# Depthwise convolution of both images on TensorE, by band matrices over image rows, before the first attention

## The chip, the cores and the metric

The kernel runs on one core of a Trainium2 chip. The metric is the device time in microseconds (us) from start to end of one launch: the median of 3 runs. Five engines work side by side, each on its own stream of instructions: TensorE (PE: matrix products, with its weight loads shown apart as PEld), VectorE (DVE), ScalarE (ACT), GpSimd (POOL) and SyncE (SP), which here issues all DMA transfers. They meet through semaphores.

## The reference

The input is two images `x` of 64 channels by 96 x 96 pixels in float32. Each is normalized over all its values, convolved channel by channel with the sum of a 3x3, a 5x5 and a 7x7 kernel, gated, projected, added to itself, normalized again, and passed through a full softmax attention over its 9216 pixels.

```
h = group_norm1(x, n1_g, n1_b)
f = dwconv(h, w3, b3) + dwconv(h, w5, b5) + dwconv(h, w7, b7)
g = sigmoid(conv1x1(f, gate_w, gate_b))
x = x + conv1x1(f * g, proj_w, proj_b)
h = group_norm1(x, n2_g, n2_b)
q, k, v = conv1x1(h, q_w, q_b), conv1x1(h, k_w, k_b), conv1x1(h, v_w, v_b)
attn = softmax(einsum("bnc,bcm->bnm", q, k) * C ** -0.5)
return x + einsum("bnm,bmc->bnc", attn, v)
```

## The kernel before, in words

Partition 64 h + c holds channel c of the upper (h = 0) or lower (h = 1) half of an image, 4608 pixels. There is no scheduler: every engine's program is written out by hand, engine by engine, and the order of the code is the order on the engine. SP's queue too is in written order, and a wait in it holds back all transfers behind it.

The program has these stages:

- **Prologue.** SP loads image 0, the parameters (`prm`) and the weight matrices. DVE takes the statistics (`x_stats`, L816) and computes the scale and shift (`norm`, L691 to L707); ACT (`pad_half`, L569) and DVE (L823) write the normalized image with a border of zeros into `hp`.
- **Convolution of image 0.** The three kernels are one 7x7 kernel of 49 taps. DVE adds up 17 taps (L844, L846). PE does 32 (`tap_sums`, L1045): diagonal 32x32 matrices `diag`, one for each tap and each group of 32 partitions, 16 of them side by side in the array (4 row groups x 4 column groups), over 10 chunks of 480 or 384 pixels. ACT moves each chunk's four partial sums out (L589), `fold_sums` (L1056) adds them up on PE, ACT takes the result out (L580), DVE adds it to its own (L832).
- **Gate to attention.** Nine chunks of 512 pixels go through gate (L1075), sigmoid (ACT L604), product (POOL L461), projection (L1092) and sum (DVE L862); then come the second statistics, h (ACT L608, DVE L877), the matrices Q, K and V (L1125, L1119), and 36 looks for the row maxima of the first query block (PE L956, DVE L714). The first of these looks waits for `QM`, a transfer on SP's queue. In the same stretch image 1 is loaded, its statistics are taken on DVE and it is normalized into `hp` (L569); ACT ends the stretch with the first tap of image 1 (L639).
- **Attention.** There are 18 query blocks of 512 queries in an image, and 36 key pairs (`p`) in a block. For a pair PE makes 1024 scores per partition in two PSUM banks (`scores`, L940): six matmuls of fp16 keys on queries (high by high, low by high, high by low), and two of `one16` on the third query row that subtract the row's maximum. ACT takes the exponential (L490). PE weighs V with it (L949), POOL and DVE add up E's two halves (L413, L730), and PE and DVE look ahead for the next block's maxima (L956, L714). At the end of a block DVE moves its sum out (`sums_out`, L737), once per block. In the image named in `SEEDED` (image 1), ACT writes the maxima into the odd pair's score banks beforehand (`seed`, L528, for 17 of the 36 pairs), and PE then leaves out the two `one16` matmuls of that pair.
- **Convolution of image 1, during the attention of image 0.** ACT multiplies a strip of `hp` by a tap (`make_tap`, L536), POOL adds it to `f` (`add_tap`, L427), about 20 such units in a block. In the last block DVE does 28 units by itself (`late_tap`, L774). The gate of image 1 waits for the last of them.

```
            def is_seeded(b, p):

                return b in SEEDED and p % 2 == 1 and p >= 3
```

## Time and profile before

| | before |
|---|---|
| median of 3 runs | 3034.27 us (3029.96 to 3035.54) |
| the profiled execution: its time, its span | 3029.67 us, 3027.9 us |
| granted TensorE clock, mean | 0.986 |
| busy in the span: PE, DVE, ACT, POOL | 2883.5, 2666.0, 2179.2, 2237.5 us |
| first gate matmul of image 0 | 158.29 us after the start |
| first scores of image 0, of image 1 | 251.09, 1717.06 us |

The span is the time from the first to the last instruction of the profiled execution. The stages are best told apart by instructions that occur once in each of them: the first gate matmul, the first scores, the copy that ends a block.

### The profile page before, as it was taken

What the parts mean: (1) busy time and instruction counts of PE and PEld (TensorE: products, weight loads), DVE (VectorE), ACT (ScalarE), POOL (GpSimd) and SP (SyncE); (2) the same over time, 40 slices, a digit from 0 to 9 for tenths busy, and PEclk for the clock granted to TensorE, in tenths of its full rate; (3) what the DMA queues carried; (4) which work ended last, traced back from release to release, by engine and by line L of the source; (5) the groups of instructions that cost most, each with busy time, mean ns of one, the idle gap of its engine ahead of it and who ended that gap; (6) DMA issues with size and microseconds to landing.
All of it is one profiled execution on the core that took longest, in us unless ns stands there. A gap on an engine that the chain in (4) does not pass through costs nothing.

```text
span 3027.9 us, 56969 instructions
## 1 busy us (share of the span) xinstructions
PE 2883.5 (95%) x20913; PEld 984.0 (32%) x20913; DVE 2666.0 (88%) x3096; ACT 2179.2 (72%) x2442; POOL 2237.5 (74%) x1754
## 2 busy tenths in 40 slices
PE   5878999999999999999997899999999999999998
PEld 2323333333333333333332333333333333333332
DVE  8577899999999999999987899999999999999994
ACT  1156677777777777777764678888888888888887
POOL 1045999999999999999996466666666666666666
PEclk9889999999999999999998999999999999999999
DMA  1020000000000000000001100000000000000000
GB/s 38 3 72 8 8 10 10 10 10 10 10 10 10 10 10 10 10 10 10 8 5 26 24 8 10 10 10 10 10 10 10 10 10 10 10 10 10 10 12 4
DMA packets 30978, 37.16 MB, mean 12 GB/s; under 512 B 6896, under 2 KB 29936, under 8 KB 30064
## 3 DMA queue, kind: packets, MB, share of 16 engines
q1 hardware_dynamic: 30704, 33.56, 4.6%
q8 instruction: 165, 2.70, 0.4%
q14 instruction: 109, 0.89, 0.1%
HBM read 9.94 MB, written 9.44 MB: 6 GB/s over the span
## 4 chain that ended last, share of the span: by engine, by line
PE 75%; DVE 7%; issue 7%; POOL 5%; ACT 4%; DMA 1%; SPq 0%; POOLq 0%; ACTq 0%; DVEq 0%
PE ps L949 32%; PE ps L940 29%; PE ps L956 10%; POOL accA L413 5%; DVE mxp L714 4%; PE ps L1045 3%; DVE ps L730 1%; ACT E L490 1%; ACT tapped L536 1%; PE ps L972 0%; ACT QQ L589 0%; DVE accB L737 0%; PE ps L1125 0%; ACT QS L520 0%; DVE ps L727 0%
## 5 line engine op out<-in xcount | busy, mean ns | idle before, releaser
L413 POOL TENSOR_TENSOR accA<-accA,E 128x512 f32<-128x512 f32 x1224 | 1574.5, 1286 | 458.9 <-ACT E L490 384.3
L490 ACT ACTIVATE E<-ps,bnd 128x1024 f32<-128x1024 f32 x1296 | 1391.0, 1110 | 566.4 <-PE ps L940 469.8
L714 DVE TENSOR_REDUCE mxp<-ps 128x1 f32<-128x1024 f32 x1296 | 1573.8, 1218 | 215.8 <-PE ps L956 191.8
L949 PE MATMUL ps<-E,x 128*64 128x512 f32 x5184 | 1268.2, 605 | 0.5 <-ACT pvb L500 0.5
L940 PE MATMUL ps<-QS,KK 64*128 64x512 f16 x7776 | 1056.4, 377 | 14.0 <-ACT mseed L521 10.1
L730 DVE TENSOR_TENSOR ps<-ps,E 128x512 f32<-128x512 f32 x1260 | 869.0, 690 | 46.6 <-ACT E L490 46.3
L956 PE MATMUL ps<-KK,QM 64*128 64x512 f16 x2592 | 500.8, 383 | 20.7 <-DVE mxp L714 17.6
L940 PEld LDWEIGHTS ps<-QS,KK 64*128 64x128 f16 x7776 | 374.0, 94 | 437.2 <-ACT E L490 24.8
L427 POOL TENSOR_TENSOR f<-f,tapped 128x576 f32<-128x576 f32 x356 | 505.3, 1420 | 0.0
L949 PEld LDWEIGHTS ps<-E,x 128*64 128x64 f32 x5184 | 310.8, 136 | 550.5 <-issue 394.9
L940 PE MATMUL ps<-QS,one 64*128 64x512 f16 x1980 | 377.4, 377 | 0.0
L956 PEld LDWEIGHTS ps<-KK,QM 64*128 64x128 f16 x2592 | 125.4, 93 | 693.4 <-DVE mxp L714 564.9
L528 ACT ACTIVATE ps<-mseed 128x1024 f32<-128x1024 f32 x306 | 314.6, 1028 | 28.9 <-ACT E L490 1.1
L536 ACT ACTIVATE tapped<-hp,prm 128x576 f32<-128x576 f32 x356 | 274.9, 772 | 0.0
L940 PEld LDWEIGHTS ps<-QS,one 64*128 64x128 f16 x1980 | 97.3, 94 | 117.5 <-issue 1.3
L461 POOL TENSOR_TENSOR f<-f,E 128x512 f32<-128x512 f32 x18 | 23.0, 1289 | 149.3 <-ACT E L604 149.3
L1045 PE MATMUL ps<-hp,KK 32*32 32x480 f32 (+1 forms) x2560 | 94.7, 637 | 27.6 <-ACT x L580 19.8
L418 POOL TENSOR_TENSOR accA<-E 128x512 f32<-128x512 f32 x36 | 46.8, 1300 | 97.7 <-ACT E L490 97.7
L589 ACT ACTIVATE QQ<-ps 128x480 f32<-128x480 f32 (+1 forms) x40 | 18.9, 559 | 102.2 <-PE ps L1045 102.2
L746 DVE RECIPROCAL rec<-rsum 128x64 f32<-128x64 f32 x144 | 77.3, 541 | 11.4 <-issue 8.5
L846 DVE SCALAR_TENSOR_TENSOR f<-hp,prm,f 128x4608 f32<-128x4608 f32 x16 | 80.3, 5019 | 0.6
L1045 PEld LDWEIGHTS ps<-hp,KK 32*32 32x32 f32 x2560 | 49.9, 109 | 70.8 <-issue 33.0
(105 smaller groups left out, 855.6 us busy)
## 6 DMA issues: line engine op xcount, KB each, us to landing
QS<-QQ SPq DMA_DIRECT2D x144, 64.0 KB, 2.0
x_scratch<-x SPq DMA_DIRECT2D x4, 1152.0 KB, 13.2
QM<-QQ SPq DMA_DIRECT2D x72, 64.0 KB, 2.0
xst<-x_scratch SPq DMA_DIRECT2D x72, 64.0 KB, 2.2
out<-ot SPq DMA_DIRECT2D x72, 64.0 KB, 2.0
xs<-in_x SPq DMA_DIRECT2D x2, 720.0 KB, 8.8
xs<-in_x SPq DMA_DIRECT2D x2, 648.0 KB, 5.9
xs<-in_x SPq DMA_DIRECT2D x2, 576.0 KB, 10.8
```

The lines of the kernel that those rows point to most:

```text
L413: nc.gpsimd.tensor_tensor(accA[:, n % 2, :], accA[:, n % 2, :], e, ALU.add).then_inc(adda_free, 1)
L427: nc.gpsimd.tensor_tensor(to, to, tapped[:, u % NTAPPED, :], ALU.add).then_inc(tap_added, 1)
L490: nc.scalar.activation(flat(E[:, slot_of(n % 2, p), :, :]), flat(ps[:, S_BANK + 2 * buf:S_BANK + 2 * buf + 2, :]), ACT.Exp, scale=bnd[:, 6 ...
L528: nc.scalar.activation(ps[:, S_BANK + 2:S_BANK + 4, :], mseed[:].unsqueeze(1).to_broadcast([P, 2, CH]), ACT.Copy).then_inc(seeded, 1)
L536: nc.scalar.activation(tapped[:, u % NTAPPED, :].rearrange("p (y x) -> p y x", x=W), window(t, s * SROWS, SROWS), ACT.Copy, scale=wc[:, t: ...
L714: nc.vector.reduce_max(flat(mxp[:])[:, v:v + 1], flat(ps[:, bank:bank + 2, :]), AX.X).then_inc(mx_free, 1)
L730: nc.vector.tensor_tensor(ps[:, SUM_BANK, :], ps[:, SUM_BANK, :], e, ALU.add).then_inc(addb_free, 1)
L846: chain(nc.vector.scalar_tensor_tensor(out=f3, in0=window(t, 0, HR), scalar=wc[:, t:t + 1], in1=f3, op0=ALU.mult, op1=ALU.add))
L940: a = nc.tensor.matmul(ps[:, S_BANK + 2 * (p % 2) + t, :], of[rows], QS[rows, par, part, :], start=(k == 0 and seeds is None), stop=(k == ...
L949: a = nc.tensor.matmul(ps[C * t:C * t + C, ACC_BANK, :], V[:, t, p, :], E[:, slot_of(par, p), t, :], start=(p == 0), stop=(p == NPAIR - 1) ...
L956: a = nc.tensor.matmul(ps[:, bank + t, :], QM[rows, half, qt * P:(qt + 1) * P], KH[rows, kc * CH:(kc + 1) * CH], start=True, stop=True)
L1045: a = nc.tensor.matmul(ps[GRP * g:GRP * g + GRP, NGRP * (c % 2) + r, 0:CROWS[c] * W].rearrange("p (y x) -> p y x", x=W), diag[rows, t, :], ...
```

## The change

The convolution of both images is moved ahead of everything else and is done on PE alone.

- The image comes in a second layout, made by the host (`x_rows`): image rows on partitions, in four windows of 24 rows with 3 rows more on each side, a window in each group of 32 partitions; channels and columns lie along the free axis (`xr`, 64 x 102 values per image and partition).
- For each channel and each of the 7 tap columns PE builds a band matrix of 32 x 24 (`bands`): 26 matmuls of 448 columns, moved out by ACT in 8 steps (`take_bands`). The bias and the effect of the border are a row of it.
- The first statistics of both images are taken on `xr` (`row_stats`, 16 bn_stats of 384 values each), and ACT normalizes `xr` in place, 8 sets of 8 channels per image (`normalize_rows`).
- `convolve(s)` does 8 channels of both images at once: 224 matmuls of 192 columns, 16 side by side in the array; there are 8 sets. DVE moves each set out (`take_convolved`, 1536 values per partition), SP writes it to DRAM (`put_convolved`, 4 transfers of 24 partitions, 1536 bytes a piece) and reads it back in the old layout (`get_convolved`, 4 transfers per image, each into 4 partitions, 384 bytes a piece). Image 0's are read back as the sets come, image 1's in one go during the attention of image 0 (32 transfers).
- `make_tap`, `add_tap`, `late_tap`, `tap_sums`, `fold_sums`, `hp`, `diag` and the parts of the prologue that feed them are gone, and so are image 1's statistics and normalization between image 0's gate and attention. POOL takes the sum and the scaling of the result of a block in image 0 too, as it did in image 1.
- `SEEDED` names both images.
- Several buffers share memory now (`arena`, `arena2`); the attention's E, Q, K and V lie where `xr` and `bands` were.

```
-SEEDED = (1,)
+SEEDED = (0, 1)
...
+            def put_convolved(s):
+
+                sp.wait_ge(conv_out, s + 1)
+                for k in range(COLS):
+                    sp.dma_start(f_dram[s, k].rearrange("(g r) k b x -> r g (k b x)", g=WINDOWS),
+                                 evac[GRP * k:GRP * k + WROWS, s % 2, :, :]).then_inc(f_out[s % 2], 16)
+
+            def get_convolved(b, s):
+
+                for half in (0, 1):
+                    for k in (0, 1):
+                        c = C * half + CSET * s + COLS * k
+                        sp.dma_start(f[c:c + COLS, :].rearrange("c (y x) -> c y x", x=W),
+                                     f_dram[s, :, HR * half:HR * half + HR, k, b, :]).then_inc(f_in, 16)
...
+            load_rows(1)
+            sp.wait_ge(wsum_ready, 1)
             load_x(0)
...
+            for s in range(NSET):
+                put_convolved(s)
+                if s:
+                    sp.wait_ge(f_out[(s - 1) % 2], 64 * ((s - 1) // 2 + 1))
+                    get_convolved(0, s - 1)
+            sp.wait_ge(f_out[(NSET - 1) % 2], 64 * (NSET // 2))
+            get_convolved(0, NSET - 1)
...
                 attend(b, 0, 1, False)
+                if b + 1 < B:
+                    sp.wait_ge(v_ps, NCH * (b + 1))
+                    for s in range(NSET):
+                        get_convolved(b + 1, s)
...
-                    if b + 1 < B and p >= 2:
-                        for u in units_of(j, p):
-                            make_tap(u)
...
+            for i in range(BAND_GROUPS):
+                take_bands(i)
+                if i == BAND_GROUPS - 3:
+                    root(0)
...
+            for s in range(NSET):
+                normalize_rows(0, s)
+            root(1)
+            act.wait_ge(aff_ready, 2)
+            for s in range(NSET):
+                normalize_rows(1, s)
...
+            def take_convolved(s):
+
+                dve.wait_ge(conv_ps, s + 1)
+                if s >= 2:
+                    dve.wait_ge(f_out[s % 2], 64 * (s // 2))
+                nc.vector.tensor_copy(evac[:, s % 2, :, :], ps[:, 4 * (s % 2):4 * (s % 2) + 4, 0:2 * B * W]
+                                      ).then_inc(conv_out, 1)
...
+            joint_kernel()
+            row_stats(0)
+            weight_norms()
+            row_stats(1)
+            for s in range(NSET):
+                take_convolved(s)
...
+            def convolve(s):
+
+                pe.wait_ge(xr_ready, NSET + s + 1)
+                if s >= 2:
+                    pe.wait_ge(conv_out, s - 1)
+                for k in (0, 1):
+                    for dx in range(KW):
+                        for g in range(WINDOWS):
+                            rows = slice(GRP * g, GRP * g + GRP)
+                            for h in range(COLS):
+                                c = CSET * s + COLS * k + h
+                                a = nc.tensor.matmul(
+                                    ps[GRP * h:GRP * h + WROWS, 4 * (s % 2) + g, k * B * W:(k + 1) * B * W].rearrange(
+                                        "p (b x) -> p b x", b=B),
+                                    bands[rows, c * KW + dx, :], xr[rows, :, c, dx:dx + W],
+                                    start=(dx == 0), stop=(dx == KW - 1), tile_position=(GRP * g, GRP * h))
+                a.then_inc(conv_ps, 1)
...
-                if b:
-                    pe.wait_ge(tap_added, len(POOL_UNITS))
-                    pe.wait_ge(late_added, len(DVE_UNITS))
+                pe.wait_ge(f_in, 16 * 4 * NSET * (b + 1))
                 gate(0)
```

How the instructions stand on the engines, at the places where the order changes (no times are in these rows). On PE, from the first instruction of the program, before (`L1045` is the convolution, `x192` that many matmuls in a row):

```order
L918 MATMUL ps<-ident,E 128x128 x5
L924 MATMUL ps<-mv,ones 128x2
L926 MATMUL ps<-dev,ones 128x1
L1045 MATMUL ps<-hp,KK 32x480 x192
L1056 MATMUL ps<-QQ,fold 32x480 x4
```

And with the change (`L1005` and `L1011` build the bands, `L896` and `L898` are the statistics of image 0, then of image 1, `L1034` is the convolution, `L1052` the gate):

```order
L1005 MATMUL ps<-f 128x448 x2
L1011 MATMUL ps<-f 128x448 x18
L896 MATMUL ps<-mv,core 128x2
L898 MATMUL ps<-dev,core 128x1
L1011 MATMUL ps<-f 128x448 x6
L890 MATMUL ps<-ident,f 128x128 x5
L896 MATMUL ps<-mv,core 128x2
L898 MATMUL ps<-dev,core 128x1
L1034 MATMUL ps<-arena 24x192 x1792
L1052 MATMUL ps<-f,wT 128x512 x3
```

The statistics of image 0 stand behind 20 of the 26 band matmuls now, and the convolution behind the statistics of both images. (A float32 matmul is one row here and two instructions in the trace, but for the five transposes.)

On SP, from the start of the program, with the change (`L307` the kernels, `L287` a quarter of an image in rows, `L281` image 0 in the old layout, `L293` a set to DRAM, `L301` a set back):

```order
L307 DMA xs<-in_conv_w 8x1792 x2
L287 DMA arena<-in_x_rows 128x1632 x4
L309 DMA prm<-in_per_channel 128x7
L312 DMA f<-in_matrices 64x5x64 x2
L287 DMA arena<-in_x_rows 128x1632 x4
L281 DMA xs<-in_x 64x4608 x2
L293 DMA f_scratch<-arena 24x4x384 x8
L301 DMA f<-f_scratch 4x48x96 x4
L293 DMA f_scratch<-arena 24x4x384 x4
L301 DMA f<-f_scratch 4x48x96 x4
```

Two sets are written out before the first one is read back; from then on writing and reading take turns. Before, nothing of the convolution went through this queue.

On ACT, in a middle block of image 0's attention, before (`L490` the exponentials, `L536` a tap of image 1):

```order
L536 ACTIVATE tapped<-hp,prm 128x576
L490 ACTIVATE E<-ps,bnd 128x1024 x2
L536 ACTIVATE tapped<-hp,prm 128x576
L490 ACTIVATE E<-ps,bnd 128x1024
L536 ACTIVATE tapped<-hp,prm 128x576
```

And with the change (`L504` the exponentials, `L542` a seed):

```order
L542 ACTIVATE ps<-mseed 128x1024
L504 ACTIVATE arena<-ps,bnd 128x1024 x2
L542 ACTIVATE ps<-mseed 128x1024
L504 ACTIVATE arena<-ps,bnd 128x1024 x2
L542 ACTIVATE ps<-mseed 128x1024
```

The taps have gone and a seed stands before every odd pair from the fourth on, as in image 1 before.

## Rows read from the trace of the kernel before

**Rows 1.** The page: busy time by engine, and the last chain by line.

```profile
PE 2883.5 (95%) x20913; PEld 984.0 (32%) x20913; DVE 2666.0 (88%) x3096; ACT 2179.2 (72%) x2442; POOL 2237.5 (74%) x1754
...
PE ps L949 32%; PE ps L940 29%; PE ps L956 10%; POOL accA L413 5%; DVE mxp L714 4%; PE ps L1045 3%; DVE ps L730 1%; ACT E L490 1%; ACT tapped L536 1%; PE ps L972 0%; ACT QQ L589 0%; DVE accB L737 0%; PE ps L1125 0%; ACT QS L520 0%; DVE ps L727 0%
```

**Rows 2.** The chain in order of time (start, us, what): each image's first scores.

```profile
251.09 3.60 PE ps L940 x16
...
1717.06 3.61 PE ps L940 x16
```

**Rows 3.** Line L737 in each image (count: shortest/median/longest ns, first and last start).

```profile
L737 DVE COPY accB<-ps x18: 678/680/691, 334.4 to 1625.6; 128x512 f32<-128x512 f32 x18
...
L737 DVE COPY accB<-ps x18: 680/682/692, 1797.6 to 3018.1; 128x512 f32<-128x512 f32 x18
```

**Rows 4.** Windows of a block of each image: us, busy (instructions) by engine, clock, DMA.

```profile
408.50:484.70 76.20, 74.80 (x512) 25.03 (x508) 69.99 (x80) 54.94 (x65) 74.34 (x58) 1.00 0.04 10
2087.60:2159.70 72.10, 71.87 (x484) 23.66 (x482) 66.61 (x80) 58.82 (x62) 47.24 (x39) 1.00 0.04 10
```

**Rows 5.** Groups in these two windows (busy, mean ns, idle before): one of image 0, two of image 1.

```profile
L940 PE MATMUL ps<-QS,one 64*128 64x512 f16 x72 | 13.7, 376 | 0.0
...
L528 ACT ACTIVATE ps<-mseed 128x1024 f32<-128x1024 f32 x18 | 18.5, 1028 | 1.7
...
L940 PE MATMUL ps<-QS,one 64*128 64x512 f16 x38 | 7.2, 376 | 0.0
```

**Rows 6.** Timeline from image 0's gate to its attention (start, us, what, [idle before]).

```profile
158.29 2.84 PE L1075 MATMUL ps<-f,wT 128*128 128x512 f32 x6 [0.61 <-ACT x L580]
...
184.94 2.10 ACT L608 ACTIVATE f<-x,aff 128x2048 f32<-128x2048 f32 x1 [1.58 <-DVE aff L707]
...
200.50 1.22 DVE L714 TENSOR_REDUCE mxp<-ps 128x1 f32<-128x1024 f32 x1
...
244.28 4.23 ACT L639 ACTIVATE f<-hp,bsum,prm 128x4608 f32<-128x4608 f32 x1
```

**Rows 7.** Timeline from image 1's gate to its row maxima.

```profile
1629.62 3.75 PE L1075 MATMUL ps<-f,wT 128*128 128x512 f32 x4 [7.12 <-POOL f L427]
...
1634.25 0.38 ACT L507 ACTIVATE rsum<-ps 128x256 f32<-128x256 f32 x1 [10.12 <-PE ps L972]
...
1664.18 2.09 ACT L608 ACTIVATE f<-x,aff 128x2048 f32<-128x2048 f32 x1 [1.59 <-DVE aff L707]
...
1673.12 7.05 DVE L714 TENSOR_REDUCE mxp<-ps 128x1 f32<-128x1024 f32 x6 [5.26 <-PE ps L956]
```

**Rows 8.** Timeline of PE alone, half a chunk of 480 and one of 384 columns.

```profile
47.73 4.28 PE L1045 MATMUL ps<-hp,KK 32*32 32x480 f32 x128
...
139.87 3.64 PE L1045 MATMUL ps<-hp,KK 32*32 32x384 f32 x128
```

**Rows 9.** Timeline of the prologue.

```profile
0.87 2.50 SPq L304 DMA_DIRECT2D xs<-in_x  x4
...
2.19 4.69 POOL L396 MEMSET hp<- 128x5508 f32 x1
...
18.04 4.83 DVE L816 BATCH_NORM_STATS2 bn<-xs 128x6 f32<-128x512 f32 x8
...
27.39 5.38 DVE L823 TENSOR_SCALAR hp<-xs,aff 64x4896 f32<-64x4896 f32 x1
27.45 4.52 ACT L569 ACTIVATE hp<-xs,aff 64x4896 f32<-64x4896 f32 x1 [1.66 <-DVE aff L707]
```

**Rows 10.** DMA in 0 to 20, 14.7 to 15.5, 190.9 to 196.5 us; last, the page's issues.

```profile
DMA packets 1264, 2.72 MB, mean 136 GB/s; under 512 B 1008, under 2 KB 1008, under 8 KB 1072
...
q1 hardware_dynamic: 1264, 2.72, 66.2%
...
DMA packets 411, 0.08 MB, mean 104 GB/s; under 512 B 411, under 2 KB 411, under 8 KB 411
...
q1 hardware_dynamic: 411, 0.08, 61.3%
...
q1 hardware_dynamic: 157, 2.32, 107.8%
...
QS<-QQ SPq DMA_DIRECT2D x144, 64.0 KB, 2.0
```

More of the change, by code:

```diff
@@ L35 @@
 H_ACT = 4
-TAPS = 49
-STRIPS = 8
-SROWS = HR // STRIPS
-NTAPPED = 5
+KW = 7
+PAD = KW // 2
+WINDOWS, GRP = 4, 32
+WROWS = H // WINDOWS
+WIN = WROWS + 2 * PAD
+MASK_ROW = WIN
+XW = W + 2 * PAD
+COLS = 4
+CSET = 2 * COLS
+NSET = C // CSET
+QUARTERS = 4
+BAND_ROWS = 3
+BAND_GROUPS = WROWS // BAND_ROWS
+TAP_COLS = C * KW
+BETA_ROW, BIAS_ROW = 32, 39
+K_ROWS = BIAS_ROW + 1
 AHEAD = 4
@@ L69, with program @@
 M_ROW = 1.0 / (ONE * 64)
[L72 removed]
+def program(nc, x, x_rows, conv_w, per_channel, matrices, out):
     with ExitStack() as ctx:
@@ L269, in slot_of @@
             return (NPAIR * par + p) % NSLOT
-        def units_of(j, p):
-            first = sum(UNITS[:j])
-            return range(first + UNITS[j] * (p - 2) // (NPAIR - 2), first + UNITS[j] * (p - 1) // (NPAIR - 2))
         def is_seeded(b, p):
@@ L1066, in _ @@
+            for s in range(NSET):
+                convolve(s)
+            pe.wait_ge(conv_out, NSET)
             for b in range(B):
@@ L1070, in gate @@
                     n = NCH * b + c
-                    if b == 0:
-                        pe.wait_ge(f_added, next(k for k in range(CCH + 1) if CROW0[k] * W >= (c + 1) * CH))
                     if c >= 3:
```

453 lines of the change are left out of this document (187 added, 266 removed).

## The prediction

> **What bounds the kernel now.** I read the page first: PE is busy for 95% of the span, and the chain that ended last runs through its lines L949, L940 and L956 for 71% of it, while the convolution of image 0 (L1045) makes 3% [rows 1]. So a change is worth what it takes off PE in the attention, and what it takes off the stretches ahead of it in which PE has little to do. The chain in order of time gives the first scores of the two images, 251.09 and 1717.06 us [rows 2], and the copy that ends each block gives the last block of image 0 at 1625.6 and of image 1 at 3018.1 [rows 3]. So the attention of image 0 takes 1374.5 us and that of image 1 takes 1301.1. The reader is to see this difference of 73.4 us, 4 us in each of 18 blocks. The windows of one block each show why: 76.2 us against 72.1, PE full in both (74.8 and 71.9 busy), and POOL at 74.3 of 76.2 in image 0 but at 47.2 of 72.1 in image 1 [rows 4].
>
> **The change part by part.** Five stretches make the span. I price each with the change; T is the time of the first gate matmul.
>
> *Attention of image 0.* The taps leave ACT and POOL, and 17 seeds a block come in. In image 0 the `one16` matmuls number 72 a block, 13.7 us of PE's busy time; in image 1 they are 38 in a window and 7.2 us [rows 5]. As two run side by side, that busy time is about what the path loses, though PE waits elsewhere for some of it. The seeds cost ACT 18.5 us a block [rows 5], where it has 76.2 - 54.9 = 21.3 us free and gives up its taps besides [rows 4]. With the change the code of a block of image 0 is that of image 1, POOL's share included, so I take image 1's time whole: **1301.1 us**, 73.4 less. The reading back of image 1's convolution falls into this stretch: 32 transfers on SP, issued at 2.50 / 4 = 0.6 us each [rows 9], so 20 us. SP issues them from about the end of block 0, and its next duty is due when the scores of block 1 are through, some 72 us later; below I price the transfers at 8 x 7.3 = 58 us, so they are hidden. Were they to last over 72 us, the queries of later blocks would stand behind them.
>
> *Gate to h of image 0* (L1075 to L608): 184.94 - 158.29 = 26.7 us before [rows 6]. PE comes to it now after waiting for transfers. Image 1's gate also follows such a wait of 7.12 us, and there four matmuls took 3.75 us where six had taken 2.84, and the stretch took 1664.18 - 1629.62 = 34.6 [rows 6, 7], part of it for the row sums. I take the middle, **30.5 us**.
>
> *From h of image 0 to its scores:* 251.09 - 184.94 = 66.2 us before; in image 1 it is 1717.06 - 1664.18 = 52.9 [rows 2, 6, 7]. Image 1 has none of the statistics, the two normalizations and the last tap (4.23 us [rows 6]) that image 0 carries, and with the change image 0 has none either. The first look comes 15.6 us after h in image 0 and 8.9 in image 1 [rows 6, 7]; as image 1 is still loaded there, beside the first queries' transfer, I keep the 15.6, and take 43.9 from image 1 for the rest: **59.5 us**.
>
> *Between the images:* 1717.06 - 1625.6 = 91.5 us before. The gate's wait of 7.12 us for the last tap on POOL goes, and with it the row sums that stand behind the gate on PE: ACT copies them at 1634.25, 8.7 us after the last block [rows 7]. What is late next is POOL's total, which needs only its last addition and DVE's copy; I let the copy of the row sums come 3 us after the block, and another 1.3 us from matmuls that no longer start slowly. **84.5 us**, 7 less.
>
> *Attention of image 1 and the end:* unchanged, 3027.9 - 1717.06 = **1310.8 us**.
>
> *Prologue up to T.* The bands need POOL's patterns: a memset of 5508 values took 4.69 us [rows 9], so one of 3072 takes 2.6; the select over 3072 values has no row, from the same 2.6 up to three times that, and I take 5. With the small operations of POOL and DVE the bands begin at 13 us (10 to 18). The gate's six instructions of 512 columns in 2.84 us [rows 6] give 0.39 us for 448; image 0's statistics stand behind 40 such: 28.5 us. The scale takes 27.39 - 22.87 = 4.5 us [rows 9]. DVE then takes the statistics of image 1 (16 x 0.45 us, from 8 in 4.83 [rows 9]) and its scale, to about 46. The data are not late: a load moves 2.72 MB in 66.2% of 16 engines' 20 us [rows 10], 12.8 bytes per ns and engine, so each image's 3.34 MB take 16 us. ACT normalizes 8 sets of 768 values of image 0 at 0.9 us each (4.52 us for 4896 [rows 9]) and is ready at about the same time. The convolution begins at **48 us**.
>
> It has 8 x 448 = 3584 instructions. Half a chunk of 480 columns took 4.28 us for 128, of 384 columns 3.64 [rows 8]: 33.4 and 28.4 ns each, 0.052 ns per column. For 192 columns that gives 18.4, the last one's latency included; I take 17 ns, 7.6 us a set, 61 us in all. The bounds are 28.4 ns (no gain from shorter ones) and, by columns alone, 11.
>
> Each set then goes to DRAM and back. Packets of 256 and 4 bytes took 61.3% of 16 x 0.8 us for 411, 19 ns each, 10 bytes per ns [rows 10], so a piece of 384 bytes takes 38 ns. Stores move 24 bytes per ns and engine (2.32 MB in 107.8% of 16 x 5.6 us [rows 10]), so one of 1536 takes 64. What no row shows is over how many engines a transfer of few partitions is spread, as all those before have 64 or 128. The ends are 16 engines and one. I take the geometric middle, 4 for the reading back, one for each partition that it fills, and 12 for the writing out of 24. Then the busiest engines have 768 / 4 x 38 ns = 7.3 us for reading and 384 / 12 x 64 ns = 2.05 us for writing, 9.4 us a set against PE's 7.6: the transfers set the pace. The first set is read from 69 us on (two sets are written first: 48 + 15.2, DVE's copy 1.7, issue 2.4, transfer 1.5), and then 8 x 7.3 + 6 x 2.05 + 1.5 to land: **T = 141 us**, against 158.3.
>
> The Trainium skill ("DMA: Bandwidth & Descriptors", section "Why a DMA increments its semaphore by 16 and not by 1") says that a transfer is spread over the largest number of engines up to 16 that divides the slowest dimension of both sides. That would be 4 for the reading and 12 for the writing. No run shown here tests it.
>
> The sum: 141 + 30.5 + 59.5 + 1301.1 + 84.5 + 1310.8 = 2927.4 us of span, against 3027.9. The profiled execution took 1.8 us more than its span, and the median of the runs is 4.6 above that: **2934 us** for the median, 3.3% less.
>
> **The rivals.**
>
> - *The transfers are spread evenly.* Then PE sets the pace: 48 + 61 + 1.7 for the copy, and 2.4 of issue and 2.0 of landing [rows 10] twice: T = 119.5, the time 2912. Every transfer of before was spread so; none was so narrow.
> - *PE's matmuls don't get cheaper with fewer columns.* At 28.4 ns [rows 8] the convolution takes 102 us and ends at 150. The last set's writing then stands ahead of two readings: 150 + 4.1 + 14.6 + 1.8 = 171, the time 2964. The two pitches in the rows speak against it, but both are for long matmuls. The Trainium skill ("TensorE: Matmul & The Clock Gate", section "Wait — 56ns, not 53.3ns?") gives a floor of about 25 ns from start to start. By it the convolution would take 90 us and the whole 2953; the rows' lower pitch, 28.4, is still above it.
> - *Small pieces cost more.* At 60 ns instead of 38 a set takes 11.5 + 2.05 us on the busiest engines: T = 175, the time 2968.
> - *The seeds bring nothing in image 0,* since something of image 0 alone makes its blocks long: 73 us more, 3007. That POOL has 1.9 us free in 76.2 there, and the code is the same afterwards, speaks against it.
> - *Slower than before:* the reading back goes through a single engine. Then a set takes 768 x 38 ns = 29 us and T = 316, the time 3109, and image 1's 233 us hold up queries besides. It decides from T = 241 on, which is 19.9 us a set for reading, 104 ns a piece on four engines.
>
> **How the numbers follow.** Chances: the forecast 0.45 (2915 to 2955 by itself), even spread 0.20, small pieces 0.15, no shorter matmuls 0.13, no seeds' gain 0.03, single engine 0.03, other 0.01. The range reaches from 2900, the even spread with a prologue some 12 us shorter, to 2980, small pieces or long matmuls with a late start of the bands. A measurement of this kernel can tell 0.2% from no change. All cases but the single engine end well below that: faster 0.96, same 0.01, slower 0.03.
>
> **What would show it.** Blocks of image 0 at 72.3 us between the copies that end them; the first scores of image 0 at about 231 us; the convolution from 48 us with starts 17 ns apart; a DMA share near 0.25 while sets are read back, and the gate 30 us after the last convolution matmul. A queries' transfer that lands tens of us late in blocks 2 to 4 would show that the reading back of image 1 is not hidden. The prediction is wrong if PE waits inside the convolution, if the bands start after 20 us, or if image 0's blocks stay above 74 us.

## The result and the profile after

The changed kernel takes 2982.45 us in the median of 4 runs (2981.14 to 2984.29), the one before 3032.11 (4 runs, 3027.42 to 3035.54; the 3034.27 above is the median of three of them): a ratio of 0.9838, 95% interval 0.9821 to 0.9855. The forecast was 2934 us with a range up to 2980. The change makes the kernel 49.7 us faster, half of what was said, and the time lies 2.45 us above the range.

The page of the changed kernel, its busy times, its last chain by line, and the group of the convolution's matmuls (out<-in, partitions x elements, count, busy us, mean ns, idle us before them):

```profile
PE 2831.4 (95%) x21297; PEld 971.8 (33%) x21297; DVE 2506.4 (84%) x3038; ACT 2258.7 (76%) x2362; POOL 1767.1 (59%) x1436
...
PE ps L921 37%; PE ps L912 31%; PE ps L928 11%; DVE mxp L734 4%; PE ps L1034 2%; PE ps L1011 1%; DVE arena L757 1%; DVE ps L747 1%; ACT arena L504 1%; PE ps L944 1%; DVE ps L750 0%; ACT rsum L521 0%; DVE bn L825 0%; DVE arena L835 0%; DVE x_max L826 0%
...
L1034 PE MATMUL ps<-arena 32*24 32x192 f32 x3584 | 74.2, 376 | 43.0 <-issue 33.2
```

POOL has gone from 2237.5 to 1767.1 us busy and DVE from 2666.0 to 2506.4 [rows 1]; PE is still full for 95% of a shorter span. "issue" in the third line is the surprise: PE waits 33.2 us inside the convolution for nothing that the profile shows.

The chain in order of time, in two pieces, up to image 0's first scores and at image 1's:

```profile
13.47 3.32 PE ps L1005 x4
16.79 26.88 PE ps L1011 x36
45.41 9.27 PE ps L1011 x12
54.70 3.54 ACT arena L574
60.48 7.40 ACT arena L567 x8
70.72 6.23 PE ps L1034 x253
...
191.59 5.58 DMA f<-f_scratch
197.30 4.49 PE ps L1052 x6
224.81 2.10 ACT f L605
...
283.78 3.61 PE ps L912 x16
...
1669.87 3.61 PE ps L912 x16
```

The copies that end the blocks (line L757; L737 before), of image 0 and of image 1 (count, shortest/median/longest ns, first and last start):

```profile
L757 DVE COPY arena<-ps x18: 678/680/691, 364.4 to 1584.5; 128x512 f32<-128x512 f32 x18
...
L757 DVE COPY arena<-ps x18: 678/680/691, 1750.5 to 2970.9; 128x512 f32<-128x512 f32 x18
```

Cut at the same places as the prediction, the span of 2980.6 us is 53.2 more than the 2927.4 forecast:

| stretch | forecast | measured | off by |
|---|---|---|---|
| start to first convolution matmul | 48 | 70.7 | +22.7 |
| convolution on PE | 61 | 107.6 | +46.6 |
| its end to the first gate matmul | 32 | 19.0 | -13.0 |
| gate to h, image 0 | 30.5 | 27.5 | -3.0 |
| h to first scores | 59.5 | 59.0 | -0.5 |
| attention of image 0 | 1301.1 | 1300.7 | -0.4 |
| between the images | 84.5 | 85.4 | +0.9 |
| attention of image 1 and end | 1310.8 | 1310.7 | -0.1 |

The 6.4 us between span and median were 1.85 this time, so the sum came out 48.5 us low. Image 0's attention gives back its 73 us to within a microsecond, but the first gate matmul, which came at 158.29 before [rows 6], comes at 197.3: 39 us of the gain are spent ahead of it. Both large misses lie ahead of 178.3 us. The windows of the convolution and of the wait behind it (us, busy (instructions) by engine, granted clock, DMA share, GB/s):

```profile
70.70:178.30 107.60, 74.22 (x3584) 52.65 (x3584) 12.30 (x7) 7.66 (x8) 0.00 (x0) 0.87 0.29 59
178.30:197.30 19.00, 0.02 (x1) 0.03 (x1) 1.76 (x1) 0.00 (x0) 0.00 (x0) 0.55 0.31 63
```

### The profile page after: what moved, and what is told of

Its sections match the earlier page's. It is cut to its first block, busy times and chain, and to the rows that moved or that the text cites. A ratio compares the mean times of both kernels' runs of the same rounds, so it can differ in the third digit from the quotient of the medians.

```text
span 2980.6 us, 57612 instructions
## 1 busy us (share of the span) xinstructions
PE 2831.4 (95%) x21297; PEld 971.8 (33%) x21297; DVE 2506.4 (84%) x3038; ACT 2258.7 (76%) x2362; POOL 1767.1 (59%) x1436
## 4 chain that ended last, share of the span: by engine, by line
PE 85%; DVE 8%; issue 4%; ACT 2%; DMA 0%; SPq 0%; POOL 0%; POOLq 0%; DVEq 0%; ACTq 0%
PE ps L921 37%; PE ps L912 31%; PE ps L928 11%; DVE mxp L734 4%; PE ps L1034 2%; PE ps L1011 1%; DVE arena L757 1%; DVE ps L747 1%; ACT arena L504 1%; PE ps L944 1%; DVE ps L750 0%; ACT rsum L521 0%; DVE bn L825 0%; DVE arena L835 0%; DVE x_max L826 0%
## 5 line engine op out<-in xcount | busy, mean ns | idle before, releaser
L440 POOL TENSOR_TENSOR arena<-arena 128x512 f32<-128x512 f32 x1224 | 1556.8, 1272 | 810.5 <-ACT arena L504 730.5
L504 ACT ACTIVATE arena<-ps,bnd 128x1024 f32<-128x1024 f32 x1296 | 1373.0, 1110 | 415.6 <-PE ps L912 345.0
L921 PE MATMUL ps<-arena 128*64 128x512 f32 x5184 | 1268.4, 605 | 1.0 <-ACT pvb L514 1.0
L912 PE MATMUL ps<-arena 64*128 64x512 f16 x7776 | 1058.0, 378 | 11.5 <-ACT rsum L521 5.9
L750 DVE TENSOR_TENSOR ps<-ps,arena 128x512 f32<-128x512 f32 x1260 | 868.9, 690 | 74.8 <-ACT arena L504 74.8
L542 ACT ACTIVATE ps<-mseed 128x1024 f32<-128x1024 f32 x612 | 629.1, 1028 | 57.1 <-ACT arena L504 1.5
L928 PE MATMUL ps<-arena,QM 64*128 64x512 f16 x2592 | 501.4, 383 | 18.4 <-DVE mxp L734 10.2
L912 PEld LDWEIGHTS ps<-arena 64*128 64x128 f16 x7776 | 372.7, 94 | 440.6 <-issue 33.2
L921 PEld LDWEIGHTS ps<-arena 128*64 128x64 f32 x5184 | 311.0, 136 | 510.7 <-issue 354.8
L912 PE MATMUL ps<-arena,one 64*128 64x512 f16 x1368 | 261.6, 378 | 0.0
L445 POOL TENSOR_TENSOR arena<-arena 128x512 f32<-128x512 f32 x36 | 45.9, 1276 | 141.1 <-ACT arena L504 141.1
L1034 PE MATMUL ps<-arena 32*24 32x192 f32 x3584 | 74.2, 376 | 43.0 <-issue 33.2
L1034 PEld LDWEIGHTS ps<-arena 32*24 32x24 f32 x3584 | 52.7, 102 | 64.2 <-issue 55.7
```

Of the source, the lines that this page charges most:

```text
L440: nc.gpsimd.tensor_tensor(accA[:, n % 2, :], accA[:, n % 2, :], e, ALU.add).then_inc(adda_free, 1)
L445: nc.gpsimd.tensor_tensor(accA[:, n % 2, :], E[:, slot_of(n % 2, 0), 0, :], E[:, slot_of(n % 2, 1), 0, :], ALU.add).then_inc(adda_free, 2)
L504: nc.scalar.activation(flat(E[:, slot_of(n % 2, p), :, :]), flat(ps[:, S_BANK + 2 * buf:S_BANK + 2 * buf + 2, :]), ACT.Exp, scale=bnd[:, 6 ...
L542: nc.scalar.activation(ps[:, S_BANK + 2:S_BANK + 4, :], mseed[:].unsqueeze(1).to_broadcast([P, 2, CH]), ACT.Copy).then_inc(seeded, 1)
L750: nc.vector.tensor_tensor(ps[:, SUM_BANK, :], ps[:, SUM_BANK, :], e, ALU.add).then_inc(addb_free, 1)
L912: a = nc.tensor.matmul(ps[:, S_BANK + 2 * (p % 2) + t, :], of[rows], QS[rows, par, part, :], start=(k == 0 and seeds is None), stop=(k == ...
```

## The experiments

**What holds the convolution.** PE's timeline at its start (start, us, what, [idle before]), and below it what the DMA queues carried from 70.7 to 178.3 us (packets, MB, share of 16 engines):

```profile
70.72 6.23 PE L1034 MATMUL ps<-arena 32*24 32x192 f32 x283 [9.61 <-ACT arena L567]
77.61 2.29 PE L1034 MATMUL ps<-arena 32*24 32x192 f32 x128 [0.65 <-issue]
81.61 2.32 PE L1034 MATMUL ps<-arena 32*24 32x192 f32 x128 [1.71 <-issue]
85.34 2.29 PE L1034 MATMUL ps<-arena 32*24 32x192 f32 x128 [1.41 <-issue]
89.89 2.69 PE L1034 MATMUL ps<-arena 32*24 32x192 f32 x128 [2.26 <-issue]
```
```profile
q1 hardware_dynamic: 7689, 5.89, 27.2%
q8 instruction: 28, 0.46, 1.8%
```

PE works in bursts of 128 matmuls, most of them at 2.29 / 128 = 17.9 ns each, and stands still between them for 0.7 to 2.3 us here (0.3 to 2.8 over the whole convolution). In the same stretch the queue that carries instructions brought 28 packets, 0.46 MB / 28 = 16.4 KB each, and 3584 matmuls with their 3584 weight loads are 7168 instructions, 256 to a packet. So one theory is that the instructions arrive too slowly: 107.6 / 28 = 3.84 us for each packet. The rivals are PE's own work per column, and the clock. The first experiment halves the columns of each matmul (it leaves out image 1's convolution); the second halves the matmuls, each with twice the columns (half of the channels then use another channel's kernel). `...` stands for code left out, and the indentation is reduced.

```diff
-  ps[GRP * h:GRP * h + WROWS, 4 * (s % 2) + g, k * B * W:(k + 1) * B * W]...,
-  bands[rows, c * KW + dx, :], xr[rows, :, c, dx:dx + W],
+  ps[GRP * h:GRP * h + WROWS, 4 * (s % 2) + g, k * B * W:k * B * W + W],
+  bands[rows, c * KW + dx, :], xr[rows, 0, c, dx:dx + W],
```
```diff
-                for k in (0, 1):
+                for k in (0,):
...
-  bands[rows, c * KW + dx, :], xr[rows, :, c, dx:dx + W],
+  bands[rows, c * KW + dx, :],
+  xr[rows, :, c:c + COLS + 1:COLS, dx:dx + W].rearrange("p b k x -> p k b x"),
```

> The changed kernel, but each convolution matmul streams the 96 columns of image 0 alone; image 1's convolution is left out, the number of instructions is the same. With the change unaltered the convolution runs from 70.7 to 178.3 us, 107.6 us, in bursts of 128 matmul instructions (2.29 us each) with 1.0 to 2.3 us between them. Theory A (PE runs out of instructions: it goes through 128 weight loads and 128 matmuls, and the next block of instructions isn't there yet): the convolution keeps 100 to 108 us, the bursts get shorter and the gaps longer. Theory B (the time is that of the columns, at the granted clock): it falls to 55 to 75 us. Theory C (waits for DVE's copy or the transfers set the gaps): it stays too, but the gaps lie at the ends of sets (every 448 instructions), not every 128.

> The changed kernel, but each convolution matmul streams 384 columns, those of two channels with the bands of the first, and there are half as many matmuls; so half of the channels are convolved with another channel's kernel. The columns streamed are the same in sum. Theory A (instructions run out every 128 matmul instructions): half as many blocks, the convolution takes 52 to 62 us instead of 107.6, with small gaps, as 128 such matmuls take 3.64 us of themselves. Theory B (columns at the granted clock): it stays near 107 us. Theory C (the transfers of a set set the pace): it falls no lower than 8 times what a set's transfers take, 75 us or more.

The windows of the convolution, half the columns first, then half the matmuls:

```profile
70.70:177.60 106.90, 65.64 (x3584) 50.18 (x3584) 12.30 (x7) 7.66 (x8) 0.00 (x0) 1.00 0.30 59
```
```profile
70.70:125.50 54.80, 51.15 (x1792) 32.65 (x1792) 12.30 (x7) 7.66 (x8) 0.00 (x0) 1.00 0.41 92
```

Half the columns leave the time as it was (106.9 us, the kernel at 2982.4); half the instructions with the same columns take half the time (54.8 us, the kernel at 2938.55). Each is a single run, and both times are theory A's. The second decides: the columns in sum and the transfers are those of the changed kernel, so neither holds the convolution at 107.6 us. The first does not decide by itself. Theory A had its bursts shorter, and they were not (2.33 us): PE ran at its lower level there, 1.2 GHz, so half the columns met half the clock.

The 1.00 in both windows is no reading of that. In the trace the first record of the clock is a rise, at 74.4 us in the changed kernel, 75.1 with half the matmuls and 199.8 with half the columns, and up to it the profile prints 1.00. The time of a weight load agrees (shortest/median/longest ns): with half the columns it is that of the changed kernel from 92 to 98 us, where the granted clock is 0.50, and not that from 99 to 118 us, where it is 1.00. The lines are the loads in this order, the windows of the two stretches, and a burst of each.

```profile
L1034 PEld LDWEIGHTS ps<-arena x3584: 107/111/159, 70.7 to 177.1; 32*24 32x24 f32 x200
...
L1034 PEld LDWEIGHTS ps<-arena x160: 107/111/159, 93.6 to 97.9; 32*24 32x24 f32 x160
...
L1034 PEld LDWEIGHTS ps<-arena x571: 92/95/99, 99.0 to 115.1; 32*24 32x24 f32 x191
```
```profile
92.00:98.00 6.00, 4.56 (x181) 2.73 (x160) 1.37 (x1) 0.00 (x0) 0.00 (x0) 0.50 0.01 3
99.00:118.00 19.00, 10.45 (x589) 7.45 (x571) 1.76 (x1) 0.00 (x0) 0.00 (x0) 1.00 0.40 85
```
```profile
93.61 3.61 PE L1034 MATMUL ps<-arena 32*24 32x192 f32 x128 [1.04 <-issue]
...
101.35 2.29 PE L1034 MATMUL ps<-arena 32*24 32x192 f32 x128 [1.13 <-issue]
```

So the changed kernel itself separates the clock from the supply. At 0.50 a burst fills 3.61 us, at 1.00 it takes 2.29, and the next one starts 4.0 us after it either way (at 97.62 and 105.35 us). The fp16 variants below say the same: 54.6 to 56.1 us at a granted clock of 0.50 to 0.55, for as many instructions as took 54.8 us here, at the upper level from 75.1 us on. The number of instructions sets the time, at 3.8 to 3.9 us for 256.

The records of the instruction queue show how. In the changed kernel a packet takes 0.9 to 1.4 us, each burst after the first starts 1.2 to 1.6 us after a packet has ended, and the next packet begins 1.0 to 2.6 us after the burst has, never while another is under way: packets from 75.31 to 76.25 and from 79.16 to 80.04 us, bursts at 77.61 and 81.61. These three times make up the round of 3.84 us, and none of them is PE's work on columns. Why no packet is asked for earlier stays open.

**Where the attention's gain comes from.** The seeds in image 0 were put into the kernel before, and taken out of the changed one:

```diff
-SEEDED = (1,)
+SEEDED = (0, 1)
```

> The kernel before, with the seeds in both images' attention and nothing else of the change; image 1's taps stay in image 0's attention. Theory A (the matmuls left out are what shortens a block, and ACT, with 54.9 of 76.2 us busy, has room for 18.5 us of seeds): blocks of image 0 go from 76.4 to 72 to 73 us, the whole is 60 to 75 us faster. Theory B (the taps on POOL and ACT lengthen the blocks as much as the matmuls do): with seeds on top ACT is full to 73.4 us and POOL to 74.3, and blocks stay at 74.5 to 77 us; the whole is 0 to 35 us faster.

> The changed kernel with the seeds in image 1 alone, as before. Theory A (the matmuls left out shorten a block): blocks of image 0 take 75.8 to 76.4 us, the whole is 65 to 75 us slower than the changed kernel, so it is slower than the kernel before by 15 to 25 us. Theory B (the taps' leaving shortens blocks by itself): blocks of 73 to 75 us, and the whole lies 15 to 50 us above the changed kernel.

The first takes 3020.87 us, ratio 0.9964 (0.9952 to 0.9976), the second 3031.28, ratio 1.0002 (0.9991 to 1.0014). A block of image 0 takes 76.0 and 75.2 us in them, against 76.4 before and 72.3 with both parts. So 0.4 and 1.2 us apart, but 4.1 together. The same 900 us inside image 0's attention, in the kernel before, with the seeds alone, without the taps alone, and with both, show why:

```profile
400.00:1300.00 900.00, 889.89 (x6082) 298.74 (x6084) 823.78 (x956) 650.50 (x763) 865.28 (x668) 1.00 0.04 10
```
```profile
400.00:1300.00 900.00, 866.07 (x5710) 279.19 (x5707) 822.27 (x961) 849.27 (x967) 870.74 (x672) 1.00 0.04 10
```
```profile
400.00:1300.00 900.00, 900.00 (x6180) 302.55 (x6178) 814.12 (x945) 499.40 (x527) 562.78 (x455) 1.00 0.05 11
```
```profile
400.00:1300.00 900.00, 897.29 (x6002) 294.61 (x6000) 832.21 (x985) 734.66 (x758) 585.91 (x474) 1.00 0.05 11
```

Busy times stand for PE, PEld, DVE, ACT and POOL in that order. Before, PE (890) and POOL (865) are both nearly full. With seeds alone PE has less to do but waits for 34 us, most of it for ACT's seeds (11.5), DVE's maxima (8.9) and ACT's copies of the row sums (7.3), while ACT (849) and POOL (871) are nearly full. With the taps alone gone POOL falls to 563, but PE is busy for all of the 900 us. Only both together lower both bounds; which of ACT and POOL holds the first variant was not separated.

**What holds the start of the convolution.** PE works on the bands from 13.47 us on, each of its 448-column instructions 0.747 us after the last, where 0.39 was forecast from the gate's rows, and behind each group of six ACT copies it from PSUM in 3.53 us. That pace is TensorE's lower level, 1.2 GHz, and the 1.00 that the profile prints for this stretch lies ahead of the first record of the clock. Four edits go at this. The first lets the band matmuls read all 128 rows (the added ones are zero) instead of 40:

```diff
-  shifts[0:K_ROWS, BAND_ROWS * i + k, :, :].rearrange("p g i -> p (g i)"), wsum[0:K_ROWS, :],
+  shifts[:, BAND_ROWS * i + k, :, :].rearrange("p g i -> p (g i)"), wsum[:],
```

> The changed kernel, but the 26 band matmuls read 128 rows of patterns and kernels instead of 40; the added rows are zero. In the changed kernel each of their instructions of 448 columns takes 0.747 us from 13.5 us on to the end at 54 us, the pace of 1.2 GHz, though PE has nearly no gap. Theory A (the rows at work count for what PE's clock is granted, and 40 of 128 are too few): the pace falls to 0.37 us a few us after the start, and ACT's copies of 3.53 us a group set the stage; image 0's statistics at 36 to 40 us instead of 43.6. Theory B (rows don't matter; it is the idle time before or the kind of matmul): 0.747 us throughout, nothing changes.

2971.91 us in one run, 10.5 less. PE's timeline at the bands, of the changed kernel and then of this one:

```profile
13.47 3.32 PE L1005 MATMUL ps<-f 40*128 40x448 f32 x4 [13.47 <-DVE f L675]
16.59 15.88 PE L1011 MATMUL ps<-f 40*128 40x448 f32 x21
```
```profile
13.48 3.32 PE L1005 MATMUL ps<-f 128*128 128x448 f32 x4 [13.48 <-DVE f L675]
16.60 5.34 PE L1011 MATMUL ps<-f 128*128 128x448 f32 x12
23.30 2.52 PE L1011 MATMUL ps<-f 128*128 128x448 f32 x6 [1.36 <-ACT arena L574]
26.66 2.52 PE L1011 MATMUL ps<-f 128*128 128x448 f32 x6 [0.84 <-ACT arena L574]
```

In the first, 21 instructions follow each other every 0.75 us with no idle time, and they keep that pace until the bands' end. In the second the pace nearly doubles after some 4 us (12 in 5.34, then 6 in 2.52 us), and the trace has its first record of a rise of the clock at 17.9 us, 4.4 us after the bands' start; PE begins to wait for ACT's copies. The convolution starts at 60.8 us instead of 70.7. Columns and order are the same; more rows of the array at work is what differs.

The second rearranges the prologue: statistics of image 0 earlier, VectorE takes every other copy, ACT normalizes image 0 between its copies, and SyncE reads each set back as soon as it is written.

```diff
+                if i == 1:
+                    stats(0, core)
                 if i == BAND_GROUPS - 3:
-                    stats(0, core)
+                    stats(2, core)
...
+            def take_bands(i):
+
+                dve.wait_ge(bands_ps, i + 1)
+                bank = 4 * (i % 2)
+                nc.vector.tensor_copy(bands[:, :, BAND_ROWS * i:BAND_ROWS * i + BAND_ROWS].rearrange("p m r -> p r m"),
+                                      ps[:, bank:bank + BAND_ROWS, 0:TAP_COLS]).then_inc(bands_out[1], 1)
...
                 put_convolved(s)
-                if s:
-                    sp.wait_ge(f_out[(s - 1) % 2], 64 * ((s - 1) // 2 + 1))
-                    get_convolved(0, s - 1)
+                sp.wait_ge(f_out[s % 2], 64 * (s // 2 + 1))
+                get_convolved(0, s)
```

> The changed kernel with another order ahead of the gate: image 0's statistics on PE behind the second group of bands instead of the sixth, image 1's behind the sixth; DVE moves every second group of bands; ACT normalizes image 0 between its groups; SP reads each set back before it waits for the next one. Theory A (the start of the convolution hangs on the chain of copies, statistics and normalizations and not on PE): the convolution starts at 54 to 60 us instead of 70.7, still takes 100 to 107 us, and the end of it to the gate falls from 19.0 to 14 to 17 us; the whole is 13 to 22 us faster than the changed kernel. Theory B (PE at 1.2 GHz sets the start): it starts at 62 us or later and the gain is under 10 us.

2976.28 us, ratio 0.9819 (0.9802 to 0.9835): only 6 us, theory B. The convolution starts at 66.7 us instead of 70.7. PE at its lower pace now ends the bands at 60.8 us, where it ended them at 54.7 before this edit, since both statistics stand among them with waits for VectorE of up to 3.5 us; what the shorter way behind the bands gives is mostly lost there. A copy takes 3.51 us on VectorE too.

The third holds bands and normalized rows as fp16, so that a matmul of the code, which in fp32 stands in the trace as two loads and two matmuls (3584 for 1792), becomes one of each:

```diff
-        bands = arena[:, N_XR:].rearrange("p (m r) -> p m r", r=WROWS)
+        bands = arena[:, N_XR:N_XR + N_BANDS // 2].bitcast(F16).rearrange("p (m r) -> p m r", r=WROWS)
+        xr16 = arena[:, N_XR + N_BANDS // 2:].bitcast(F16).rearrange("p (b c x) -> p b c x", b=B, c=C)
```

> The changed kernel with the bands and the normalized rows in fp16, so that a convolution matmul of the program is one weight load and one matmul instruction instead of two of each; the convolution is less exact. Theory A (PE runs out of instructions every 128 matmuls): 1792 matmul instructions, 14 blocks, 50 to 56 us instead of 107.6, bursts of under 2.3 us and gaps as before. Theory B (array time): fp16 columns need a quarter of the time, so 15 to 35 us. Then the transfers of the sets, 8 to 9 us each on their engines, set the time of the gate: about 70.7 + 16 + 8 x 8 to 9, 150 to 160 us instead of 197.3, and the whole is 37 to 47 us faster than the changed kernel.

2950.49 us, ratio 0.9735 (0.9716 to 0.9755). The convolution takes 55.4 us, with 14 packets of instructions (3584), but starts 14 us later: ACT's copies now take 6.59 us each. (The first record of the clock is at 168.3 us here, so the convolution ran at the lower level.) The fourth, in the changed kernel otherwise, keeps the bands in the order in which PSUM holds them, so that the copy writes side by side and PE's weight loads read with a stride instead:

```diff
-        bands = arena[:, N_XR:].rearrange("p (m r) -> p m r", r=WROWS)
+        bands = arena[:, N_XR:].rearrange("p (r m) -> p m r", r=WROWS)
```

> The band matrices are kept in the order in which TensorE leaves them in PSUM (row, then tap column), so that ScalarE's copy writes side by side instead of every 96 bytes, and a convolution matmul's weight load reads its 24 columns 2688 bytes apart. Everything else is the changed kernel. Theory A (ScalarE's 3.53 us a copy is the price of writes apart; the supply of instructions still sets the convolution's pace): the copy falls to about 1.5 to 2 us; TensorE's own pace at 1.2 GHz sets the bands, so the convolution starts only 1 to 2 us earlier (last copy shorter); convolution stays at 107 us; time 2980 to 2982 us. Theory B (a weight load that reads columns far apart is slower, which shows since it comes before every matmul): bursts of 128 take clearly more than 2.29 us, the convolution 110 to 150 us; time 2985 to 3020 us. Theory C (3.53 us is the price of reading 14-bank PSUM rows and not of the writes): the copy stays above 3 us.

ACT's group of copies in the changed kernel, with fp16, and in this one:

```profile
L574 ACT ACTIVATE arena<-ps 128x1344 f32<-128x1344 f32 x8 | 28.2, 3526 | 26.4 <-PE ps L1011 26.4
```
```profile
L580 ACT ACTIVATE arena<-ps 128x1344 f16<-128x1344 f32 x8 | 49.6, 6588 | 19.2 <-PE ps L1017 19.2
```
```profile
L574 ACT ACTIVATE arena<-ps 128x1344 f32<-128x1344 f32 x8 | 10.3, 1291 | 42.0 <-PE ps L1011 42.0
```

The copy of 1344 values falls from 3.53 to 1.29 us. The weight loads do get slower by their stride, 112 to 117 ns each at a granted clock of 1.00 against 92 to 95 in the changed kernel, and a burst takes 2.37 us instead of 2.29. It does not show in the time (the convolution takes 106.4 us) because the supply of instructions sets that. The line shows the loads of this kernel from 92 to 110 us:

```profile
L1034 PEld LDWEIGHTS ps<-arena x607: 112/117/139, 92.0 to 108.1; 32*24 32x24 f32 x152
```

In this kernel the edit is worth only 1.6 us (2980.81 against 2982.45, which the measurement cannot tell from nothing), since PE's pace holds the bands.

**The narrow transfers.** Each read back was made to fill 8 partitions of `f` instead of 4, with twice as many writes of half the size and another layout in DRAM:

```diff
-                    for k in (0, 1):
-                        c = C * half + CSET * s + COLS * k
-                        sp.dma_start(f[c:c + COLS, :]..., f_dram[s, :, HR * half:HR * half + HR, k, b, :])
+                    c = C * half + CSET * s
+                    sp.dma_start(f[c:c + CSET, :]..., f_dram[s].rearrange("k h y b x -> (k h) y b x")[...])
```

> The changed kernel with the sets laid out in DRAM so that one transfer reads back 8 channels into 8 partitions (2 transfers a set and image instead of 4, the same packets of 384 bytes); writing a set out takes 8 transfers of 768-byte packets instead of 4 of 1536. In the changed kernel image 1's 32 transfers take from 363.4 to 411 us, 47.6 us, with a DMA share of 0.30. Theory A (a transfer lies on as many DMA engines as the partitions it fills allow: 4 there, 8 here): 22 to 28 us and a share near 0.55; the end of the last convolution to the gate falls from 19.0 to about 15 us, the whole by 3 to 5 us. Theory B (all 16 engines serve it, and something else such as DRAM's answer time or SP's issue limits it): 40 us or more.

The DMA view while image 1 is read back, changed kernel (363.4 to 411 us), then this one (369 to 411):

```profile
q1 hardware_dynamic: 6432, 2.49, 28.8%
```
```profile
q1 hardware_dynamic: 6432, 2.49, 52.4%
```

The share rises, but a packet is on record for 0.524 x 16 x 42 / 6432 = 55 ns instead of 0.288 x 16 x 47.6 / 6432 = 34, and the reading ends some 36 us after its start instead of 47.6. Neither theory holds in full. The share does not count engines exactly: from 369 to 400 us, while the reading runs, it is 0.65, more than 8 of 16 give unless packets' times overlap. The kernel is 4 us slower (2986.83, ratio 0.9855, 0.9835 to 0.9875): its convolution takes 113 us, and the wait after it is about the same (18.6 us). The 5.4 us more are two waits for instructions, of 4.4 and 4.2 us, at which packets of instructions came 6.6 us apart; why those were late stays open.

**Together.** Order, fp16 and full rows in one; then also the dense bands; then that with SyncE's order of the changed kernel (the last hunk of the second edit taken back).

> Three earlier variants together: the prologue's other order with the copies of the bands shared between ScalarE and VectorE, fp16 bands and image rows (half the convolution's instructions), and band matmuls that read all 128 rows. Theory A (each removes its own wait: the instruction supply, TensorE's low clock in the bands, ScalarE's turn at the copies): bands set by the copies at about 6.5 us each, four on each engine, convolution from about 66 us on, 55 us long, first gate matmul at about 147 us, time about 2932 us (2925 to 2938). Theory B (fp16 copies on both engines, with image 0's row statistics and normalisation between them, hold the start at 75 us or later): time 2940 to 2948 us, little under the fp16 variant's 2950.

> The variant of the run before with the bands kept in the order in which TensorE leaves them in PSUM, so that the fp16 copies write side by side. Theory A (writes apart are what costs 6.5 us; weight loads that read columns 1344 bytes apart cost nothing that shows): copies of 1.5 to 2 us, the start of the convolution set by the statistics of image 0 and ScalarE's normalisation, 50 to 56 us; convolution 55 us; first gate matmul at about 135 us; time 2915 to 2926 us. Theory B (weight loads with columns apart are slower): the start comes as early, but the convolution lasts 65 to 90 us, time 2930 to 2955 us.

> The variant of the run before, but with the order of the changed kernel on SyncE's queue: put set s, then read back set s-1, where the other waited for each set's writing before it read it and put the next. Theory A (in the variant before, this queue's round trip of about 12 us a set, longer than the 7 us that a set now takes on TensorE, set the time from the convolution's end to the gate: 51.5 us of waiting): the convolution stays at 49 to 104 us, the wait falls to the 25 us that the fp16 variant had, first gate matmul at about 129 us, time about 2917 us (2912 to 2922). Theory B (the transfers themselves, not the queue's order, set it): the wait stays above 40 us, time 2932 to 2945 us.

They take 2966.75 (ratio 0.9783, 0.9768 to 0.9798), 2944.91 (0.9705, 0.9692 to 0.9718) and 2916.47 us (0.9612, 0.9596 to 0.9628). The first is slower than either theory had it, and slower than the fp16 variant without the other edits: copies of 6.3 us on both engines let its convolution start only at 73.0 us, and behind its end at 129.1 the gate waited 52.5 us, so that it came at 181.5 us and not at 147. The second lies in theory B's range but not for its reason: the convolution took 54.6 us, not 65 to 90. The waits of PE in the first 200 us, of the second and of the third (line, releaser: us in total, times, longest):

```profile
PE ps L1082 <- DMA f<-f_scratch: 51.5, 1, 51.5
PE ps L1064 <- issue: 28.5, 13, 3.6
```
```profile
PE ps L1067 <- issue: 30.9, 13, 3.6
PE ps L1085 <- DMA f<-f_scratch: 24.2, 1, 24.2
```

The convolution was as early and as short as expected (49.6 to 104.2 us), but the gate then waited 51.5 us. SyncE's timeline in the second shows its round (start, us, what):

```profile
62.07 2.01 SPq L303 DMA_DIRECT2D f<-f_scratch  x4
64.83 4.80 SPq L295 DMA_DIRECT2D f_scratch<-arena  x4
73.71 2.08 SPq L303 DMA_DIRECT2D f<-f_scratch  x4
```

Write, wait until it has landed, read, write the next: 11 to 12 us a set. That hid behind PE's 13.5 us a set in fp32, and sets the pace against PE's 7 in fp16. With the old order, where set s is written before set s-1 is waited for, the wait is 24.2 us, the first gate matmul comes at 129.7, and the version is the fastest measured: 66 us below the changed kernel and 115.6 below the one before.

## Why the prediction was right and wrong, step by step

**Attention of image 0: right**, in size (1300.7 against 1301.1) and in reason: "the code of a block of image 0 is that of image 1". The rival that the seeds bring nothing falls, but in the kernel before they do bring almost nothing by themselves: the gain needs the taps to go as well. The reading back of image 1 was hidden, as said, in 47.6 us instead of 58.

**"I take 17 ns, 7.6 us a set": the step that failed.** The spacing was right, 17.9 ns inside a burst at the upper level. What failed is that the spacing was taken for the whole: nothing priced how instructions reach the engine. PE gets 256 of them in about 3.84 us, 30 ns for a matmul with its load, and the 61 us became 107.6: +46.6. The prediction's own sign of being wrong, "if PE waits inside the convolution", came with 33.2 us. The rows of before did not show it: there 128 matmuls took 4.28 or 3.64 us [rows 8], about as long as a packet. The rival "PE's matmuls don't get cheaper with fewer columns" gave 102 us for the convolution and nearly hit it, for a reason that is not the true one: inside a burst 192 columns do go at 17.9 ns and not at 28.4, and with half the instructions twice the columns fit into half the time. The Trainium skill ("TensorE: Matmul & The Clock Gate", section "Wait — 56ns, not 53.3ns?") and its floor of about 25 ns from start to start don't fit here: 128 matmuls in 2.29 us lie below it. What the Trainium skill says of the supply ("Runtime: NRT & Kernel Launch", section "Instruction fetch mechanics"), that the next block of 256 instructions is fetched while the current one runs and that crossing a block is mostly hidden, agrees with the 28 packets for 7168 instructions, but the hiding does not: 33.2 us of "issue" in 107.6.

**The start at 48 us: two terms mis-sized, +22.7.** The bands began at 13.47, as said (13). "0.39 us for 448" was the pace of the gate's matmuls at 2.4 GHz with 128 rows (2.84 / 6 x 448 / 512 gives 0.41); the bands ran at 0.747 for their whole length, and 15.2 of the 22.7 us are there when image 0's statistics come, at 43.7 instead of 28.5. With 128 rows the pace came to 0.42, and the start to 60.8. And ACT's copies of the bands had no price: at 3.53 us each they bind as soon as PE is faster. Both are shown by the runs; with both removed, in fp16 and with the prologue's other order, the convolution starts at 49.6.

**The transfers.** "4 for the reading back" fits: a share of 0.288 is near 4 of 16, and more partitions raise it; as packets' times overlap, the share does not prove the number. The Trainium skill's rule of the largest divisor up to 16 ("DMA: Bandwidth & Descriptors", section "Why a DMA increments its semaphore by 16 and not by 1") agrees with this. The 12 for the writing was not measured apart. The price of a piece was 34 ns instead of 38. The transfers did not set the pace in the changed kernel since PE was slower, so the wait behind the convolution was 19.0 instead of 32. That hid 13 us of the miss. In the fp16 variants with the changed kernel's order of transfers, where PE takes the 7 us a set of the forecast, the wait is 24.2 and 25.2.

**Between the images, gate to h:** within 3 us each.

**The range** left too little room: its upper end, 2980, is 16 us above the 2964 of the long matmuls, and the late start alone was 22.7. That the miss is only 2.45 us is luck: the profiled execution and the median lay 1.85 us above the span instead of 6.4, and the later stretches took 3 us less.

## What to carry to other kernels

Before many short instructions are put into a stretch, count them, loads and matmuls both: here PE got 256 in 3.8 us whatever they did, so a longer or rarer instruction is worth more than a narrower one. Before a granted clock of 1.00 is believed, look whether the profile has a record of the clock yet; here it printed 1.00 for the bands at the lower level. Where two engines are both nearly full, price a change by both together: two edits gave 0.4 and 1.2 us a block alone and 4.1 together. And when one wait is removed, look again at the order of the queue behind it; SyncE's order of write, wait and read cost nothing while PE took 13.5 us a set, and 27 us once it took 7.

## What the runs showed of the hardware that was not expected

- Instructions came in packets of 16.4 KB, 256 at a time. Short matmuls ran in bursts of 128 with 0.3 to 2.8 us of waiting between; 28 packets took 106.4 to 107.6 us in four kernels and 113.0 in a fifth, 14 took 54.6 to 56.1, at either level of the clock. A packet took 0.9 to 1.4 us, a burst began 1.2 to 1.6 us after one had ended, and no two were under way at once.
- Back-to-back fp32 matmuls of 448 columns with 40 rows ran at 0.747 us each, TensorE's 1.2 GHz level, for some 40 us; with 128 rows, 6 took 2.52 us after some 4 us of work.
- A copy of 1344 fp32 values from PSUM took 1.29 us on ScalarE written side by side, 3.53 written 96 bytes apart and, as fp16 written 48 bytes apart, 6.59; VectorE took 3.51 for the fp32 one and 6.30 for the fp16 one, and 1.54 for fp16 side by side.
- The profile printed a granted clock of 1.00 up to the first record of the clock, at 74.4 us in the changed kernel and 199.8 us with half the columns, though PE ran at the lower level.
- A weight load of 24 columns took 112 to 117 ns where they lie 2688 bytes apart and 92 to 95 side by side, at a granted clock of 1.00; in fp16, 1344 bytes apart, 112 to 115 against 87 to 90, at 0.50. Behind the supply of instructions it did not show.
- A 384-byte packet took 34 ns where a transfer filled 4 partitions and 55 where it filled 8; the same 6144 were read in 47.6 and in some 36 us.
